# Mixture-of-experts accumulation on VectorE put off by up to two steps, in a linear-attention block on eight cores

## The reference

```python
q = elu(x @ Wq.T + bq) + 1; k = elu(x @ Wk.T + bk) + 1; v = x @ Wv.T + bv
# per head, chunk by chunk of 128 rows, with the running sums S (64x64), z (64)
num = tril(q k^T) v + q S;  den = q . (cumsum(k) + z);  out = num / den
S += k^T v;  z += sum(k)
x1 = layernorm(x + out @ Wo.T + bo)
gates = softmax(x1 @ gate_w.T + gate_b);  top_gates, top_idx = top_k(gates, 2)
y = layernorm(x1 + sum over the two of gate * (x1 @ expert_w[e].T + expert_b[e]))
```

## Time and profile before

| | us |
|---|---|
| median of 2 runs (lowest, highest) | 2875.88 (2872.55, 2879.2) |
| the profiled execution's own time | 2881.92 |
| its span on the slowest core, core 3 | 2880.4 |
| spans of the 8 cores | 2862.8 to 2880.4 |
| mean granted TensorE clock, per core | 0.78 (of 2.4 GHz) |
| PE busy / DVE busy / ACT busy on core 3 | 1887.0 (66%) / 999.1 (35%) / 543.0 (19%) |

### The profile page before, as it was taken

The page is one execution under the profiler, slowest core; times in us unless marked ns, Lnnn a source line. Parts: engine busy times, 40 slices in busy tenths (PEclk is TensorE's granted clock), DMA queues, the critical chain, the costliest instruction groups (busy, mean ns, idle before and its releaser), DMA issues.

```text
span 2880.4 us, 26565 instructions; the slowest of 8 cores (2862.8 to 2880.4 us)
## 1 busy us (share of the span) xinstructions
PE 1887.0 (66%) x10144; PEld 900.9 (31%) x10144; DVE 999.1 (35%) x1456; ACT 543.0 (19%) x686; POOL 142.5 (5%) x265
## 2 busy tenths in 40 slices
PE   1644554854698448964499457974499545994496
PEld 0222221332243223432244223432244322442242
DVE  0233322243233423343233533344233432334333
ACT  1322111322003220122103220032101221032200
POOL 1000000000000000000000000000000000000000
PEclk8765787965799559975699668986699757995698
DMA  5540365420334113330134203340134302441131
GB/s 168 203 150 15 139 233 220 160 81 8 111 123 158 47 44 132 117 132 15 58 148 145 81 8 117 131 162 30 59 119 133 121 8 88 143 144 57 37 117 59
DMA packets 63346, 303.93 MB, mean 106 GB/s; under 512 B 8172, under 2 KB 8428, under 8 KB 43766
## 3 DMA queue, kind: packets, MB, share of 16 engines
q1 hardware_dynamic: 34326, 163.80, 16.5%
q0 software_dynamic: 28896, 138.43, 12.9%
HBM read 260.26 MB, written 41.94 MB: 105 GB/s over the span
## 4 chain that ended last, share of the span: by engine, by line
PE 52%; DVE 15%; DMA 15%; ACT 9%; issue 8%; DVEq 1%; POOL 0%; ACTq 0%; SPq 0%; POOLq 0%
PE q L912 26%; PE q L744 6%; DMA wb<-escr 5%; PE q L381 5%; DMA wb<-ewT 5%; PE q L436 3%; DMA xtl<-xT 3%; PE q L750 2%; PE q L442 2%; PE q L562 2%; ACT L835 1%; DVE x1f L764 1%; DVE S_f L634 1%; DVE x1f L897 1%; ACT wb L263 1%
## 5 line engine op out<-in xcount | busy, mean ns | idle before, releaser
L912 PE MATMUL q<-wb,x1t_bf 128*128 128x512 bf16 x4096 | 932.3, 391 | 109.5 <-DVE x1f L897 58.9
L912 PEld LDWEIGHTS q<-wb,x1t_bf 128*128 128x128 bf16 x4096 | 409.2, 100 | 632.7 <-issue 178.9
L926 DVE SCALAR_TENSOR_TENSOR x1f<-q,w_all,x1f 128x1024 f32<-128x1024 f32 x256 | 328.0, 1283 | 474.1 <-PE q L912 474.0
L381 PE MATMUL q<-xt_bf,wb 128*128 128x512 bf16 x1024 | 243.7, 396 | 134.6 <-DMA wb<-escr 48.3
L744 PE MATMUL q<-wb,attnTb 128*128 128x512 bf16 x512 | 185.4, 541 | 42.4 <-ACT attnTb L735 42.4
L404 ACT ACTIVATE etmp<-q,bqc_s 128x512 f32<-128x512 f32 x64 | 44.7, 699 | 812.5 <-PE q L381 803.6
L381 PEld LDWEIGHTS q<-xt_bf,wb 128*128 128x128 bf16 x1024 | 101.7, 101 | 271.0 <-issue 163.9
L562 PE MATMUL q<-qt_bf,ktz 128*128 128x128 bf16 x512 | 55.3, 289 | 159.7 <-DVE qtz L540 141.9
L197 POOL DMA_DIRECT2D wb<-escr x126 | 67.2, 533 | 1710.2 <-PE q L912 773.6
L764 DVE TENSOR_TENSOR x1f<-q,x0c 128x1024 f32<-128x1024 f32 x32 | 39.2, 1224 | 301.8 <-PE q L750 301.8
L805 PE MATMUL q<-id_bf,x1c_bf 128*128 128x128 bf16 x256 | 32.8, 308 | 150.1 <-ACT x1c_bf L798 150.1
(11 more groups left out here) (84 smaller groups left out, 1630.4 us busy)
## 6 DMA issues: line engine op xcount, KB each, us to landing
wb<-escr SPq DMA_DIRECT2D x70, 1024.0 KB, 5.0
wb<-escr POOLq DMA_DIRECT2D x70, 1024.0 KB, 7.1
wb<-ewT SPq DMA_DIRECT2D x16, 2048.0 KB
escr<-wb SPq DMA_DIRECT2D x12, 2048.0 KB, 7.6
xtl<-xT POOLq DMA_DIRECT2D x64, 256.0 KB, 3.2
x0c<-x POOLq DMA_DIRECT2D x32, 512.0 KB, 4.3
out<-osb POOLq DMA_DIRECT2D x32, 512.0 KB, 2.9
wb<-escr SPq DMA_DIRECT2D x56, 256.0 KB, 3.0
```

The lines of the kernel that those rows point to most:

```text
L381: fn = lambda e, src=src, k=k, f=f: e.matmul(quad[2 + (f % 4) // 2][:, ((f % 4) % 2) * 512:((f % 4) % 2 + 1) * 512], src[:, k * 1024 + f * ...
L912: fn = lambda e, src=src, k=k, c=c, qi=qi, hh=hh: e.matmul(quad[qi][:, hh * 512:(hh + 1) * 512], x1t_bf[:, c * 1024 + k * 128: c * 1024 + ...
L926: e.scalar_tensor_tensor(x1f[:, c * 1024:(c + 1) * 1024], quad[qi][:], w_all[:, c * 8 + e_i: c * 8 + e_i + 1], x1f[:, c * 1024:(c + 1) * 1 ...
```

## The change

The accumulation is no longer written behind its step's matmuls. A step now only appends an entry to the list `pend_acc`; a new function `flush_acc(keep)` writes the oldest entries' accumulations into VectorE's stream until `keep` are left. It is called in three places: in `ffn_drain` ahead of every step with `keep=1`; in `qwait`, for the entries that hold the buffer asked for and all older ones; and with `keep=0` ahead of the second layer norm. A debugging output, which the kernel doesn't make, is dropped. The instructions themselves are the same.

```diff
     def qwait(qi, halves=(0, 1)):
+        if any(p[2] == qi for p in pend_acc):
+            last = max(i for i, p in enumerate(pend_acc) if p[2] == qi)
+            flush_acc(keep=len(pend_acc) - last - 1)
         evs = []
...
+    pend_acc = []
+
+    def flush_acc(keep=0):
+        while len(pend_acc) > keep:
+            kind, c, qi, e_i, vpe = pend_acc.pop(0)
+            B.wait("DVE", "cpe", vpe)
+            if kind == "e":
+                B.wait("DVE", "cdv", w_done[c])
+            acc_wait_dve(c)
+            B.wait("DVE", "dtap", tap_guard[0])
+            if kind == "b":
+                vstt = B.op("DVE", lambda e, c=c, qi=qi: e.scalar_tensor_tensor(
+                    x1f[:, c * 1024:(c + 1) * 1024], quad[qi][:], 1.0,
+                    x1f[:, c * 1024:(c + 1) * 1024], ALU.mult, ALU.add),
+                    inc="cdv")
+            else:
...
+            stt_val[c] = vstt
+            qset(qi, (0, 1), [("cdv", vstt)])
...
     def emit_ffn_exp(s, e_i, c, qi):
...
-        B.wait("DVE", "cpe", vpe)
-        B.wait("DVE", "cdv", w_done[c])
-        acc_wait_dve(c)
-        B.wait("DVE", "dtap", tap_guard[0])
-        vstt = B.op("DVE", lambda e, c=c, qi=qi, e_i=e_i:
-                    e.scalar_tensor_tensor(
...
-        stt_val[c] = vstt
-        qset(qi, (0, 1), [("cdv", vstt)])
...
+        pend_acc.append(("e", c, qi, e_i, vpe))
...
             step = ffnq.pop(pick)
             c = step[-1]
+            flush_acc(keep=1)
             qi = ffn_qi[0]
             ffn_qi[0] ^= 1
...
             ffn_drain(pend_ln2[0])
+            flush_acc(0)
             ln2_out(pend_ln2[0])
...
                 ffn_drain(s)
+                flush_acc(0)
                 ln2_out(s)
```

More of the change, by code:

```diff
@@ L877, in acc_wait_dve @@
             B.wait("DVE", "cdv", stt_val[c])
+    pend_acc = []
[13 more added lines that the diff above has]
+            else:
+                vstt = B.op("DVE", lambda e, c=c, qi=qi, e_i=e_i:
+                            e.scalar_tensor_tensor(
+                                x1f[:, c * 1024:(c + 1) * 1024],
+                                quad[qi][:],
+                                w_all[:, c * 8 + e_i: c * 8 + e_i + 1],
+                                x1f[:, c * 1024:(c + 1) * 1024],
+                                ALU.mult, ALU.add), inc="cdv")
+            stt_val[c] = vstt
+            qset(qi, (0, 1), [("cdv", vstt)])
     def emit_ffn_bias(c, qi):
@@ L893, in emit_ffn_bias @@
                 vpe = B.op("PE", fn, inc="cpe")
-        B.wait("DVE", "cpe", vpe)
-        acc_wait_dve(c)
-        B.wait("DVE", "dtap", tap_guard[0])
-        vstt = B.op("DVE", lambda e, c=c, qi=qi: e.scalar_tensor_tensor(
-            x1f[:, c * 1024:(c + 1) * 1024], quad[qi][:], 1.0,
-            x1f[:, c * 1024:(c + 1) * 1024], ALU.mult, ALU.add), inc="cdv")
-        stt_val[c] = vstt
-        qset(qi, (0, 1), [("cdv", vstt)])
+        pend_acc.append(("b", c, qi, 0, vpe))
     def emit_ffn_exp(s, e_i, c, qi):
```

## The result

The changed kernel takes 3149.15 us (median of 11 runs; before 2878.8 in 10), a ratio of 1.0928 (95% interval 1.0914 to 1.0942): 267 us slower. I had forecast 3114 us (+238), in a range up to 3145. The direction, the places and the mechanism came as forecast; two of the sum's four terms, the clock and stage 0, were much too small.

The account below looks back on a forecast made before the run. TensorE, busy over half the span, was taken as the bound. Pauses 188 + clock 48 + stage 0 5 - given back 3 = 238 us on 2881.92: 3120, or 3114 us against the median 2875.88; range 3060 to 3145.

Parts of the forecast that it names:

- The pauses in the projections: Stages 1 to 7: TensorE waits 6.5 us behind each of three waves and 7.4 us at v, 188 us in all.
- What is given back: Waits for weights behind a new pause, such as 1.42 us in stage 1, shrink: 3 us off.
- The clock after a pause: Matmuls behind each of 28 projection pauses lose 1.7 us to a lower clock, 48 us; ends 0 and 1.8 each.
- Stage 0: Experts' steps start later behind weight casts, so the stage ends about 5 us later; bounds 0 and 14.
- the chain of loads is 3.0 us later: Stage 0: a weight cast starts 3.0 us later, so the landing at 443.24 moves to 446.2.
- the clock holds: Rival: projection pauses as forecast but full speed after each, 190 us more, 3066 us; chance 0.10.
- Stage 0 is worse: Rival: loads fall behind by two whole steps each period, 14 us instead of 5, 3123 or 3137 us; chance 0.05.
- Hidden: Rival: accumulations stay covered by two alternating buffers and VectorE's 2.17 us spare per step, 2876 us; chance 0.02.
- faster: Rival: waits at drain heads and stage 0's casts, 58.9 + 42.4 us, would go, about 2775 us; chance 0.01.
- The rule of the Trainium skill on rotating banks: Matmul groups rotating through different PSUM banks overlap emptying with the next group's matmuls; by it the change costs nothing.
- the 135 named as a sign: Expert matmuls of stages 1 to 7: 21 new waits on VectorE's accumulation of some 6.5 us, 135 us in total.

Follow-up runs that it names:

- The bare pauses: Kernel before, TensorE alone also waits in stages 1 to 7 for the first, second or last of each wave's four joins: 1.0259, 1.0413, 1.0731.
- the projections-alone kernel: Changed kernel with the deferral undone in stage 0 by writing owed accumulations ahead of each weight cast: 1.0906 against the kernel before, 260 us slower.
- the kernel with stage 0 alone: Changed kernel with the deferral undone in the projections by writing owed accumulations ahead of each wave's joins: 1.0040 against the kernel before, 11.5 us slower.
- both longer bare pauses: Kernel before, TensorE alone also waits for the second (some 3.0 us) or last (some 5.3 us) of each wave's four joins: 1.0413 and 1.0731.

## Why the prediction was right and wrong

**The pauses in the projections** were right. Worked out were three of 6.5 us and one of 7.4 in each stage. Measured as idle time they are 6.32 to 6.60 and 7.38 to 7.39 us, and each also ends the overlap of 0.16 us, so 27.3 us for a stage where I had 26.9 (the idle times alone sum to 26.7). The bare pauses show that they act through TensorE's standing still, and the projections-alone kernel that nothing else in stages 1 to 7 is needed.

**What is given back**: I took off 3 us. In stages 2 to 7 nothing came back: of the 36.4 us by which a stage grew 27.3 are pauses and 9.0 are clock. In stage 1 it was 2.4 us on core 3: the wait of 1.42 us at 552.48 is gone, and so is 0.9 us of slow matmuls which before had in that stage's first pair of steps (7.93 us). So the size of this term was about right.

**The clock after a pause** failed, as a size. The step said that a pause of 6.5 us "lies between 3.21 and 19.78, and both ends say the same. I take 1.7 us", with 1.8 as the upper end. On core 3 the 28 pauses of stages 1 to 7 lost 63 us instead of 48, 2.2 each, between 1.3 and 2.9. My upper end came from three rows, and what one pause loses scatters over a factor of two. The runs with one length each show the scatter at every length that loses at all: 1.3 to 2.9 us at 3.0, at 5.3 and at 6.4 us of pause. What the length changes is how often, 15 of 28 at 3.0 us and all at 5.3, and what stands just ahead of the pause counts too. The gate's page in the Trainium skill ("TensorE: Matmul & The Clock Gate", Part 1) calls the number of slow matmuls after a start "run-variable"; the traces agree with the scatter (8.42 and 9.50 us for equal pairs behind nearly equal pauses in one stage), and no run here shows its cause.

**Stage 0** failed by more than half: 5 us worked out, 14 measured (stage 1's first wave ends at 537.7 instead of 523.5 on core 3), and 11.5 in the kernel with stage 0 alone, whose core 3 is 8.3 us late at this place; the size is not the same in every execution. VectorE's weight casts show which step. Changed kernel, core 3:

```profile
349.97 2.29 DVE L263 CAST wb<-wb 128x4096 bf16<-128x4096 f32 x1 [5.68 <-PE q L934]
...
391.87 2.29 DVE L263 CAST wb<-wb 128x4096 bf16<-128x4096 f32 x1 [28.05 <-DMA wb<-ewT]
...
411.30 2.29 DVE L263 CAST wb<-wb 128x4096 bf16<-128x4096 f32 x1 [5.62 <-PE q L934]
...
453.48 2.29 DVE L263 CAST wb<-wb 128x4096 bf16<-128x4096 f32 x1 [28.22 <-DMA wb<-ewT]
...
472.82 2.29 DVE L263 CAST wb<-wb 128x4096 bf16<-128x4096 f32 x1 [5.62 <-PE q L934]
...
514.18 2.29 DVE L263 CAST wb<-wb 128x4096 bf16<-128x4096 f32 x1 [27.40 <-DMA wb<-ewT]
```

The short intervals, in which a cast now waits for TensorE, were worked out well: 391.87 to 411.30 and 453.48 to 472.82 are 19.4 and 19.3 us, where the earlier trace rows have 16.4 and 16.7 and I had 19.4 and 19.1. The step that failed is "the chain of loads is 3.0 us later", as a block: the long intervals, with three loads and two casts of ScalarE in each, were taken as unchanged, and they grew too, 38.8 to 42.2 and 38.3 to 41.4 us. From the first to the last of these casts the eight cores take 148.1 to 150.4 us before and 148.4 to 150.0 with the projections alone changed, but 159.0 to 164.2 in the changed kernel and 158.7 to 164.3 with stage 0 alone. So it belongs to the deferral in stage 0. On core 3's chain the three loads between the casts at 411.30 and 453.48 take 9.14, 13.94 and 7.97 us, where those between 404.42 and 443.24 took 7.59, 12.77 and 7.41. The stores of 2 MB, which are issued on the same queue (SyncE's) as these loads, take 8.6 us to land in the median instead of 7.6. Why the loads are slower in the kernels with the deferral in stage 0 stays open: I made no run for it.

**The rivals.** That the clock holds (3066) is refuted by the changed kernel's own rows, in which all 28 groups behind a pause are slow, and by both longer bare pauses. "Stage 0 is worse" took 14 us for stage 0, which is what came, but by luck: its reason, two steps (6.9 us) lost in each of two periods, isn't what the casts show, and it left the clock at 1.7. Hidden and faster fall with the 27 + 7 waits. The rule of the Trainium skill on rotating banks ("Perfetto Trace Analysis", Matmuls) would have had no loss: q0 and q1 still take turns in the changed kernel, and the loss is 9%. The trace disagrees with it as a sufficient rule.

**The sum**: 191 (pauses with their overlap) + 63 + 14 - 2 = 266 on core 3, and 265.7 is what lies between the two kernels at the transposes of stage 7; 267 was measured. Core 3's span grew by 271.3. The rest is the last drain, 117.98 instead of 112.92 us for its 512 matmuls, with a granted clock of 0.81 in part of it on cores 2 and 3 and 112.94 us on core 0; I don't put it down to the change. The forecast's 238 is 15 short at the clock, 9 at stage 0, 3 at the overlap and 1 at what it took off. The top of the range, 3145, held stage 0's 14 us, but for the clock only 28 x 1.8 = 50 us where 63 came: an end from three rows was taken as a bound. A slip without weight: 21 waits of 6.5 us are 136.5 us and not the 135 named as a sign; the trace has 135.0, with pauses of 6.4.

## What to carry to other kernels

With engines that work in order, what matters for an evacuation is not how late it may be but what stands ahead of it in its own queue: put it ahead of instructions that wait for another engine or for a DMA, and spread such instructions out (here 73 us, with eight casts moved). Two alternating buffers give one step of cover, and an evacuation written two steps late spends it all. By the runs of this kernel, price a new pause in a dense matmul stretch at its length plus about 2 us of slow matmuls when it is 5 us or longer, with 1.3 and 2.9 us as the ends, and at about 3 us of pause take the loss in a third to a half of the cases. Look for other short waits, or for small matmuls, just ahead of it: there a pause of 1.8 us lost as much.

## What the runs showed of the hardware

I had not expected the scatter of the clock's loss, nor that it depends on neighbours. A pause of 1.7 us lost 1.3 to 2.9 us in 17 of 21 cases in which a wait for weights stood four matmuls ahead of it, and nothing when it stood alone (61 cases on three cores); a pause of 1.8 us behind four one-row matmuls lost clock in 7 of 7 stages on one core and in 2 of 7 on another. At 3.0 us, 13 of 28 pauses kept 2.4 GHz. Nor had I expected that the 2 MB loads of stage 0 would take longer with the deferral there: from one cast of VectorE to the next with three loads between them it takes up to 3.8 us more on core 3.
